# Message pass of a graph network: the gathered node row is added onto the edge row by the DMA

## The reference

```
msg = relu(h[src] @ W1a.T + h[dst] @ W1b.T + edge_attr @ W1c.T + b1)
msg = msg @ W2.T + b2
agg = segment_sum(msg, src)
h_new = gru(agg, h)
```

## Time and profile before

| | |
|---|---|
| median of 3 runs | 6856.87 us (6795.88 to 6858.34) |
| the profiled execution | 6859.47 us, span 6857.5 us |
| busy over the span: TensorE matmul, weight load | 4859.2 us (71%), 3529.3 us (51%) |
| VectorE, ScalarE, GpSimd | 3972.7 us (58%), 2326.2 us (34%), 3357.2 us (49%) |
| the message stage, from first gather to last addition | 2419.7 to 3042.4 us |

### The profile page before, as it was taken

The page is one execution under the profiler, slowest core; times in us unless marked ns, Lnnn a source line. Parts: engine busy times, 40 slices in busy tenths (PEclk is TensorE's granted clock), DMA queues, the critical chain, the costliest instruction groups (busy, mean ns, idle before and its releaser), DMA issues. The chain is left out here.

```text
span 6857.5 us, 82677 instructions
## 1 busy us (share of the span) xinstructions
PE 4859.2 (71%) x21442; PEld 3529.3 (51%) x21443; DVE 3972.7 (58%) x11544; ACT 2326.2 (34%) x4547; POOL 3357.2 (49%) x3181
## 2 busy tenths in 40 slices
PE   1998687888459867779656777559985655566594
PEld 0665566666346644546435555436654444444384
DVE  9302677777856677755437777843454445444534
ACT  0333555555212233322125555433322222221132
POOL 4776666666434367740135555100007773775053
PEclk9999889888679989889557777769997777777597
DMA  2554433333344656640333222100013332333424
GB/s 45 141 139 106 120 104 103 100 102 102 78 123 133 97 169 185 182 123 1 89 85 80 73 75 72 27 16 14 14 37 101 103 101 64 100 103 77 136 68 107
DMA packets 377709, 633.66 MB, mean 92 GB/s; under 512 B 130352, under 2 KB 258451, under 8 KB 376033
## 3 DMA queue, kind: packets, MB, share of 16 engines
q0 software_dynamic: 146096, 360.51, 18.7%
q1 hardware_dynamic: 231005, 263.55, 14.7%
q10 hardware_dynamic: 308, 6.40, 0.3%
HBM read 474.19 MB, written 155.98 MB: 92 GB/s over the span
## 5 line engine op out<-in xcount | busy, mean ns | idle before, releaser
L784 POOL DMA_INDIRECT conv_rows<-rows_b,index x832 | 824.8, 991 | 1134.6 <-SPq L2707 881.7
L816 DVE TENSOR_TENSOR acc<-acc,ps 125x257 f32 (+1 forms) x1664 | 702.0, 422 | 754.4 <-PE ps L2753 580.3
L2753 PE MATMUL ps<-conv_rows,conv_weight_of 128*125 128x256 f32 x1664 | 631.9, 561 | 483.2 <-DMA conv_rows<-rows_b,index 344.3
L2753 PEld LDWEIGHTS ps<-conv_rows,conv_weight_of 128*125 128x125 f32 x1664 | 475.7, 293 | 639.4 <-issue 416.8
L784 POOL DMA_INDIRECT gat_rows<-rows,index x416 | 514.0, 1236 | 298.3 <-PE ps L1099 150.8
L333 POOL DMA_INDIRECT records_src<-by_src_edge_stage,by_src_edge_slot x400 | 430.1, 1075 | 373.9 <-issue 119.8
L784 POOL DMA_INDIRECT hyp_rows<-rows,index x416 | 417.7, 1004 | 347.9 <-PE ps L2360 213.6
L784 POOL DMA_INDIRECT mpnn_rows<-rows_b,index x416 | 456.9, 1098 | 231.7 <-issue 116.0
L2741 ACT ACTIVATE conv_weight_of<-conv_onehot_b,index 128x125 f32<-128x125 bf16 x832 | 251.5, 385 | 829.3 <-DVE conv_onehot_b L2725 829.3
L499 POOL DMA_INDIRECT records_dst<-front_back,front_dst_addr x400 | 409.6, 1024 | 218.6 <-issue 133.3
L1023 ACT CAST room<-ps 125x1024 bf16<-125x1024 f32 x416 | 404.5, 1017 | 297.6 <-PE ps L1086 290.5
(11 more groups left out here) (591 smaller groups left out, 10288.6 us busy)
## 6 DMA issues: line engine op xcount, KB each, us to landing
mpnn_edge<-records_src SPq DMA_DIRECT2D x104, 512.0 KB
edge_rows<-front_edge_ring SPq DMA_DIRECT2D x100, 451.5 KB
by_src_edge_stage<-edge_rows SPq DMA_DIRECT2D x100, 451.5 KB
conv_rows<-rows_b,index POOLq DMA_INDIRECT x832
front_attr<-in_edge_attr SPq DMA_DIRECT2D x100, 112.0 KB
rows_b<-acc SPq DMA_DIRECT2D x15, 560.0 KB
second_w<-in_L_ffn_w SPq DMA_DIRECT2D x1, 8192.0 KB
slots<-mlp_y SPq DMA_DIRECT2D x56, 128.0 KB
```

The lines of the kernel that those rows point to most:

```text
L784: pool.indirect_dma_start(out=rows[:, n % U, t, :], out_offset=None, in_=table, in_offset=bass.IndirectOffsetOnAxis(ap=ends[:, n * G + t:n ...
L816: dve.tensor_tensor(here, here, S.ps[0:P, t % banks, 0:width], ALU.add).then_inc(added, 1)
L2753: pe.matmul(S.ps[0:P, t, 0:D], weight_of[:, q.slot, t, :], rows[:, q.slot, t, :], start=True, stop=True).then_inc(summed, 1)
```

## The change

The edge values are loaded straight into the ring slot `rows`, all 8 tiles of a group in one DMA of 1 MB. Once they have landed, GpSimd issues the 8 gathers with `compute_op=ALU.add`, so that each gathered row is added onto what the slot holds. `message` adds the own node's part in the slot. The buffer `edge`, the wide additions and the semaphore `joined` are gone. SyncE's load of a slot waits for `summed` of the group 4 back, as the gather did before; the gather waits for `edges_in`; message 0 of a group waits for its 8 gathers; relu waits for `messages`. The loads are written out, and no longer in a loop.

```diff
--- before.py
+++ after.py
@@ -1705,10 +1705,10 @@
                 dve.wait_ge(taken, 2)
 
         gathered = [sem(f"gathered{u}") for u in range(U)]
-        edges_in = [sem(f"edges_in{u}") for u in range(2)]
-        (go, selected, turned, turned_out, widened, products, messages, joined, rectified, summed, added, ready) = (
-            sem(x) for x in ("go", "selected", "turned", "turned_out", "widened", "products", "messages", "joined",
-                             "rectified", "summed", "added", "ready"))
+        edges_in = [sem(f"edges_in{u}") for u in range(U)]
+        (go, selected, turned, turned_out, widened, products, messages, rectified, summed, added, ready) = (
+            sem(x) for x in ("go", "selected", "turned", "turned_out", "widened", "products", "messages", "rectified",
+                             "summed", "added", "ready"))
         with nc.Block() as block, ExitStack() as ctx:
             def mb(what, shape, dt=F32):
                 return ctx.enter_context(nc.sbuf_tensor(f"mpnn_{what}", shape, dt))
@@ -1716,24 +1716,27 @@
             rows = mb("rows", [128, U, G, D + 1])
             onehot_b, onehot = mb("onehot_b", [128, 2, G, P], BF16), mb("onehot", [128, 2, G, P])
             onehot_t = mb("onehot_t", [P, 2, G, 128], BF16)
-            edge = mb("edge", [128, 2, G // 2, D])
             view = S.records["src"][0:SLOTS].rearrange("(p t) w -> p t w", p=128)
 
             PB = 4
 
             @block.sync
             def _(sp):
-                def load(q):
-                    for half in range(2):
-                        if q.since(1):
-                            sp.wait_ge(joined, 2 * q.n - 1 + half)
-                        tiles = bass.ds(q.n * G + half * (G // 2), G // 2)
-                        sp.dma_start(edge[:, half], view[:, tiles, 2:EW]).then_inc(edges_in[half], 16)
-                pipeline(sp, (0, load))
+                for n in range(GROUPS):
+                    if n >= U:
+                        sp.wait_ge(summed, (n - U + 1) * G)
+                    sp.dma_start(rows[:, n % U, :, 0:D], view[:, n * G:(n + 1) * G, 2:EW]).then_inc(edges_in[n % U], 16)
 
             @block.gpsimd
             def _(pool):
-                gather_groups(pool, ends, S.rows_b, rows[:, :, :, 0:D], summed, gathered, go)
+                for n in range(GROUPS):
+                    pool.wait_ge(edges_in[n % U], 16 * (n // U + 1))
+                    pool.sem_inc(go, 1)
+                    for t in range(G):
+                        pool.indirect_dma_start(
+                            out=rows[:, n % U, t, 0:D], out_offset=None, in_=S.rows_b,
+                            in_offset=bass.IndirectOffsetOnAxis(ap=ends[:, n * G + t:n * G + t + 1], axis=0),
+                            compute_op=ALU.add).then_inc(gathered[n % U], 16)
 
             @block.vector
             def _(dve):
@@ -1749,30 +1752,18 @@
 
                 def message(t):
                     def stage(q):
-                        half, m = t // (G // 2), t % (G // 2)
-                        if m == 0:
-                            dve.wait_ge(edges_in[half], 16 * (q.n + 1))
+                        if t == 0:
+                            dve.wait_ge(gathered[q.slot], rows_in(q))
                         dve.wait_ge(products, q.n * G + t + 1)
-                        v = edge[:, half, m, :]
+                        v = rows[:, q.slot, t, 0:D]
                         dve.tensor_tensor(v, v, S.ps[:, 2 + t % PB, 0:D], ALU.add).then_inc(messages, 1)
                     return stage
 
-                def join(half):
-                    def stage(q):
-                        if half == 0:
-                            dve.wait_ge(gathered[q.slot], rows_in(q))
-                        at = slice(half * (G // 2), (half + 1) * (G // 2))
-                        dve.wait_ge(messages, q.n * G + at.stop)
-                        v = rows[:, q.slot, at, 0:D]
-                        dve.tensor_tensor(v, v, edge[:, half], ALU.add).then_inc(joined, 1)
-                    return stage
-
                 pipeline(dve, (0, select), *(
-                    stage for half in range(2) for stage in (
-                        *(s for t in range(half * (G // 2), (half + 1) * (G // 2)) for s in (
-                            (2, message(t)),
-                            (3, lambda q, t=t: accumulate(dve, S, q, ids, D + 1, 2, summed, added, [t])))),
-                        (2, join(half)))), written_out=True)
+                    stage for t in range(G) for stage in (
+                        (2, message(t)),
+                        (3, lambda q, t=t: accumulate(dve, S, q, ids, D + 1, 2, summed, added, [t])))),
+                    written_out=True)
 
             @block.scalar
             def _(act):
@@ -1785,7 +1776,7 @@
                 def rectify(q):
                     for half in range(2):
                         t = half * (G // 2)
-                        act.wait_ge(joined, 2 * q.n + half + 1)
+                        act.wait_ge(messages, q.n * G + t + G // 2)
                         v = rows[:, q.slot, t:t + G // 2, 0:D]
                         act.activation(v, v, ACT.Relu).then_inc(rectified, 1)
```

## The result

The changed kernel takes 7031.78 us (7027.59 to 7037.88, 3 runs) against 6856.87 us: a ratio of 1.0267, 95% interval 1.0239 to 1.0296 (estimated from the single runs; the two medians alone give 1.0255). The forecast was 6920 us, +0.9%; the range to 7120 us holds the time, but the loss of 175 us is 2.8 times the 62 us forecast. The profiled execution took 7031.8 us for a span of 7030.1 us.

What follows compares the result with a forecast made beforehand. Two nearly equal loops, GpSimd's gathers and VectorE with ScalarE, bound the stage; after the change, GpSimd. Head 5 + 52 groups x 12.74 = 662.5 + tail 17.5 = 685 us against 622.6, so 6920 us; range 6815 to 7120.

Steps and rivals of the forecast that it cites:

- Added: the accumulation in the gather: GpSimd's accumulating gathers: each takes 1.20 us, between 0.95 and 1.90, so a group takes 12.74 us.
- rival B: Message stage: each row is written out twice, gather 1.90 us, 7210 us; half of the way 7015 us; chance 0.25.
- A second term: GpSimd's gathers: one a group overlaps the one-hot and takes 0.74 us more.
- The removal: VectorE's wide additions, 127 us of work: without them its loop lies under GpSimd's; stage -41.6 us at a 0.95 us gather.
- The load: GpSimd's wait for edge rows: 5 us before the first gather, nothing after group 0.
- The tail: End of the message stage after the last gathers: 17.5 us, where it was 35.2.
- The longer step: VectorE's 12.8 us step between one-hots, beside one of 11.0: read as part of TensorE's lower clock level.
- The transfers: DMA engines in the message stage: doubled gathers give a floor of 10.0 us a group, under 12.7, so no bound.
- Rival A: Message stage: accumulation is free, gather stays at 0.95 us, 42 us less, 6815 us; chance 0.30.
- C: Message stage: DMA transfers become the bound; three times as long gives 6940 us; chance 0.11 together with D.
- D: Message stage: the edge load is late in every group, 154 us if it takes 20 us; chance 0.11 together with C.
- for the second only: SBUF contention with gathers: the trace agrees for the one-hot (0.74 us), not for the wide addition (0.10 us).

Runs made afterwards that it cites:

- The forms: Changed kernel with eight gather forms in each group (accumulating or plain; 128, 125 or 64 rows; 256 or 128 columns): 7941.6 us, where the kernel before takes 7924.54.
- first: Changed kernel with plain gathers, which overwrite the edge values instead of accumulating: 6802.13 us, ratio 0.9907 to the kernel before.
- second experiment: Kernel before with the wide additions taken out, edge and own parts left out of the sum: 6806.81 us, ratio 0.9930.
- third experiment: Changed kernel with edge loads for the first four groups only: 7039.8 us, ratio 1.0275 to the kernel before.
- The widening between the relus: Kernel before, ScalarE widening the one-hots between its two relus, not after both: 6806.14 us, ratio 0.9932; on another chip 7968.72 us, ratio 1.0050.
- the sums by half: Kernel before, TensorE's first four sums of a group waiting for the first relu alone: 6872.33 us, ratio 1.0011; with the widening moved too, 6805.21 us, 0.9940.

## Why the prediction was wrong

**The step that failed is the size of "Added: the accumulation in the gather".** I took 1.20 us, from the gathers of 125 rows, as "the same instruction when it has more pieces to write out". The changed kernel's gather takes 1.541 us (median over the stage). 416 x (1.541 - 0.953) = 245 us, where the sum had 104: 141 us short. The forms show why that row was no likeness: its 0.25 us is what a plain gather gains by rows, while an accumulating one has a fixed sum of 0.46 us that no row of the trace before could show, and twice the part by rows. Both of my bounds, 0.95 and 1.90 us, held. The row between them was nearer in packets than in what costs; my rival B, "each row is written out twice", was right for the part by rows (0.105 for 0.062 us, 0.473 for 0.231) and wrong in taking the whole gather as such a part. The time lies near the 7015 us that rival B gave for half of its way, and it is this rival, a gather of over 1.30 us with a chance of 0.25, that came true. With 1.541 us in it the forecast's own sum gives 204 us more than before, 7061 us.

**A second term was too large the other way.** I gave each group 0.74 us of gather held up by the one-hot, 38 us in all. From the timelines, gather by gather: in the kernel before 51 gathers started while a one-hot was running, and took 36.6 us more than 0.953 us each in sum; in the changed kernel 20 did, with 9.3 us over 1.541 us. The gathers beside them were not held up. That is 29 us less than forecast, since the one-hots no longer came at the same place in each group of gathers: 62 + 141 - 29 = 174 us, against 175 measured.

**The rest held.** The removal: VectorE's loop fell under GpSimd's, and of 127 us of work some 50 us of time came out, with a gather at 0.95 us (first and second experiment; -41.6 forecast). That this number came so near is in part luck: in the trace of the second experiment the gathers' stretch fell by 45 us, where the sum had 29, and the tail by 8 us, where it had 18. The load: 2415.9 - 2409.8 = 6.1 us to the first gather, where it was 0.7: 5.4 us, 5 forecast; after that, 0.9 us in 400. The tail: 18.2 us, 17.5 forecast. The longer step, which I had put down to TensorE's lower level, does lie there: from 2704.5 to 2715.5 us (the step of 11.0 us) the granted clock was 1.00, from 2715.5 to 2728.4 us (the one of 12.8) it was 0.74. The transfers: no bound, though a gather's engine time went from 6.2 to 14.5 us, 2.3 times and not 2. The Trainium skill ("Collectives: The Full Stack", The bandwidth ceiling) has half the rate for an add; the trace agrees roughly, and my conclusion that this would not change the sum held, by the third experiment. A group now needs (8 x 14.5 + 56) / 16 = 10.8 us of the 16 engines, 56 us being its edge rows' share of 24.1%, and has 14.9. Rival A falls by the gather of 1.54 us, C by the third experiment, D by the first. The reading that GpSimd's and VectorE's loops were nearly equal holds too: with VectorE's idle time out, the gathers' idle time over the stage is 126.5 us, which is 0.30 us for each, so GpSimd alone binds, and 47 us come out.

**Against the wide addition I had read too little.** The sum took 0.10 us for a gather beside a wide addition, from one row. The 99 gathers that started while a wide addition was running took 23.9 us more in sum, 0.24 us each. One of my own rows shows the other end: the gather of 2984.80, which I had read for its wait only, took 1.75 us, 0.79 more, and a wide addition had begun just before it:

```profile
2984.49 1.22 DVE L1767 TENSOR_TENSOR mpnn_rows<-mpnn_rows,mpnn_edge 128x1024 f32<-128x1024 f32 x1
```

So the wide addition and the one-hot hold a gather up in the same way, and 0.10 and 0.74 us differ by how long each had still to run. The Trainium skill ("SBUF — State Buffer", Who interferes with whom) has an exclusive lock between a VectorE instruction with two SBUF inputs and a GpSimd instruction that reads SBUF. The trace agrees for both once the start is looked at, as the last section shows; the prediction's "for the second only" was wrong.

## What to carry to other kernels

Work that goes from one engine to a DMA lands on the engine that issues the DMA: ask whether that engine is the bound, and multiply its price by the number of instructions, not by bytes. An operation that the trace does not show should be priced by its bounds, and a row that resembles it in one count (here packets) is no reason for a narrow forecast between them. Where two loops are nearly equal, 127 us taken from one gave 50 us, and swapping two instructions on a third engine gave as much (0.7%) with nothing left out. The widening between the relus gained 0.7% on one chip, and 0.6% together with the sums by half on another; on a third, where the stage's clock was 0.79, it lost 0.5%. It has to be measured where it is to run.

## What the runs showed of the hardware

An accumulating gather of 128 rows holds GpSimd for 1.54 us, a plain one for 0.95. Most of the difference is a fixed sum for each instruction (0.46 us by the eight forms), and half of the bytes changed it by nothing. An accumulating DMA without indices takes 1.72 us for 1024 rows.

A gather is held up by a VectorE operation with two inputs in SBUF (the one-hot, the wide addition) only if that is already running when the gather starts, and then to its end. GpSimd and VectorE in the changed kernel:

```profile
2711.28 1.54 POOL L1736 DMA_INDIRECT mpnn_rows<-rows_b,index  x1 [0.30 <-issue]
2713.13 1.54 POOL L1736 DMA_INDIRECT mpnn_rows<-rows_b,index  x1 [0.30 <-issue]
```

```profile
2711.95 1.20 DVE L799 TENSOR_TENSOR mpnn_onehot_b<-iota,index 128x1000 bf16<-128x1000 f32 x1 [1.61 <-ACT mpnn_onehot L1786]
```

The one-hot starts at 2711.95, within the gather of 2711.28, which takes its 1.54 us; the next starts as the one-hot ends, and is not held up. In the kernel before, the one-hot of 2704.53 was running when the gather of 2704.89 started, and had 0.85 us to go: the gather took 0.73 us more. The wide addition of 2708.40 had 0.23 us to go at the gather of 2709.39, which took 0.10 more; that of 2984.49 had 0.92 us to go, and cost 0.79.

The extra is the time left less 0.13 us. In the kernel before 149 gathers started with more than 0.15 us of such an operation left, and in each the extra was 0.12 to 0.13 us less than that time; in the changed kernel's accumulating gathers it was 0.11 to 0.13 us less. A message or an accumulation has one input in SBUF and one in PSUM: 191 gathers started while one of these was running and neither of the others, and none took over 0.004 us more than 0.953. So the same two instructions cost 0 or 0.7 us by their order, and in the kernel before the one-hot cost it to 51 gathers, about one in each group.
